# A graph kernel whose matmul groups hand their semaphore updates to TensorE's sequencer

## The reference

```python
# layer 0: spline convolution
messages = jnp.einsum('ek,ei,kio->eo', basis, x[row], weight)   # basis: 9 values per edge
out = zeros.at[col].add(messages) / jnp.maximum(degree, 1.0)[:, None] + x @ root_w.T + root_b
x = _layernorm(x + out)
# layer 1: tensor product with a radial network
R = jax.nn.relu(abs_distances[:, None] @ w1 + b1) @ w2 + b2     # 384 used weights per edge
Y = spherical_harmonics(rel_vec)
msg = ...                          # einsums of R, Y and features[src]
x = _layernorm(x + zeros.at[dst].add(msg))
```

## Time and profile before

| | |
|---|---|
| median of 3 runs | 11,184.96 us (11,180.47 to 11,219.96) |
| profiled execution | 11,204.5 us is its span, from the first to the last instruction; no other time of it is given |
| TensorE busy, matmuls | 7268.4 us, 65%, 30,515 records |
| TensorE weight loads | 3770.5 us, 34%, 30,515 |
| VectorE | 5863.1 us, 52%, 14,800 |
| ScalarE | 2726.5 us, 24%, 7,061 |
| GpSimd | 5939.1 us, 53%, 6,282 |
| mean granted TensorE clock | 0.790 |

### The profile page before, as it was taken

One profiled execution on the slowest core, in us unless ns is written; L12 is line 12 of the kernel. 1 busy time (PEld: TensorE's weight loads), 2 busy tenths in 40 slices (PEclk: granted clock), 3 DMA queues, 4 the chain that ended last, 5 costly groups with the idle time before them and its releaser, 6 DMA issues. The chain is left out here.

```text
span 11204.5 us, 123807 instructions
## 1 busy us (share of the span) xinstructions
PE 7268.4 (65%) x30515; PEld 3770.5 (34%) x30515; DVE 5863.1 (52%) x14800; ACT 2726.5 (24%) x7061; POOL 5939.1 (53%) x6282
## 2 busy tenths in 40 slices
PE   5555555555555555556777777777777777777777
PEld 2222222222222222233333333333333333333334
DVE  3333333333333333335666666666666666666666
ACT  1000000000000000013333333333333333333333
POOL 5555656555555555554444445444445444444443
PEclk8777777777777777778888888888888888888887
DMA  1111111111111111112111111111111111111111
GB/s 26 13 13 13 13 13 13 13 13 13 13 13 13 13 13 13 13 22 50 43 42 42 43 42 44 42 41 43 41 42 44 43 42 41 43 43 42 43 41 38
DMA packets 640988, 332.17 MB, mean 30 GB/s; under 512 B 522497, under 2 KB 573212, under 8 KB 640718
## 3 DMA queue, kind: packets, MB, share of 16 engines
q0 software_dynamic: 200800, 205.61, 9.7%
q10 hardware_dynamic: 266000, 112.04, 4.9%
q1 hardware_dynamic: 174168, 14.29, 1.2%
HBM read 325.06 MB, written 6.40 MB: 30 GB/s over the span
## 5 line engine op out<-in xcount | busy, mean ns | idle before, releaser
L166 POOL DMA_INDIRECT rows<-table_dram,idx_a x1875 | 1778.6, 949 | 2153.3 <-DVE prods L1010 1563.6
L166 POOL DMA_INDIRECT rows<-in_x,idx_a x1890 | 1786.3, 945 | 1072.9 <-issue 547.3
L897 PE MATMUL sums_ps<-prods,hot 128*64 128x272 f32 x12500 | 1817.9, 442 | 697.3 <-DVE acc L1041 356.8
L581 PE MATMUL sums_all<-spread,hot 128*64 128x289 f32 x6250 | 2039.3, 482 | 112.4 <-DVE spread L459 75.1
L886 PE MATMUL radial_x<-w2p,hidden 128*128 128x384 f32 x3750 | 1703.5, 600 | 506.5 <-DVE prods L1010 462.2
L166 POOL DMA_INDIRECT rows<-table_dram,idx_b x1250 | 1182.4, 946 | 1000.4 <-DVE prods L1010 639.5
L166 POOL DMA_INDIRECT rows<-in_x,idx_b x1260 | 1191.0, 945 | 945.9 <-DVE spread L459 575.0
L897 PEld LDWEIGHTS sums_ps<-prods,hot 128*64 128x64 f32 x12500 | 945.2, 152 | 1589.8 <-issue 792.9
L857 ACT ACTIVATE hot<-window,rel_t 128x64 f32<-128x64 f32 x3125 | 812.8, 335 | 2373.4 <-remote 1753.2
L581 PEld LDWEIGHTS sums_all<-spread,hot 128*64 128x64 f32 x6250 | 943.6, 160 | 909.7 <-issue 472.7
L886 PEld LDWEIGHTS radial_x<-w2p,hidden 128*128 128x128 f32 x3750 | 805.3, 230 | 1072.8 <-issue 413.9
(11 more groups left out here) (148 smaller groups left out, 5749.7 us busy)
## 6 DMA issues: line engine op xcount, KB each, us to landing
dist_ab<-in_edge_weight ACTq DMA_DIRECT2D x125, 480.0 KB
dist_ab<-in_edge_weight ACTq DMA_DIRECT2D x125, 320.0 KB
rows<-in_x,idx_a POOLq DMA_INDIRECT x1890
rows<-table_dram,idx_a POOLq DMA_INDIRECT x1875
rows<-in_x,idx_b POOLq DMA_INDIRECT x1260
rows<-table_dram,idx_b POOLq DMA_INDIRECT x1250
vec_s<-in_edge_attr ACTq DMA_DIRECT2D x125, 37.5 KB
idx_a<-in_src SPq DMA_DIRECT2D x251, 7.5 KB
```

Of the source, the lines that this page charges most:

```text
L166: pool.indirect_dma_start(out=rows[u][:, j, 0:width], out_offset=None, in_=table, in_offset=bass.IndirectOffsetOnAxis(ap=idx[u // 3][:, u ...
L581: last = pe.matmul(sums_ps[s][0:WINDOW, 0:K + 1], hot[s][:, j, :], spread[s][:, j, :], start=(j == 0), stop=(j == G - 1))
L897: last = pe.matmul(sums_ps[s][k * WINDOW:(k + 1) * WINDOW, 0:HALF], hot[s][:, j, :], prods[s][:, j, MUL + 16 * k:MUL + 16 * (k + 1), :].re ...
```

## The change

In both loops the last matmul of a group loses its update. Behind each group stands a drain on TensorE, and the semaphore is updated when the drain is done. Nothing else moves: same matmuls, operands, waits and order. The set-up and the transposes between and behind the loops (lines 544 to 568, 630, 1107) keep their updates.

```diff
@@ spline_layer @@
                 for j in range(G):
-                    last = pe.matmul(sums_ps[s][0:WINDOW, 0:K + 1], hot[s][:, j, :], spread[s][:, j, :], start=(j == 0), stop=(j == G - 1))
-                last.then_inc(summed, 1)
+                    pe.matmul(sums_ps[s][0:WINDOW, 0:K + 1], hot[s][:, j, :], spread[s][:, j, :], start=(j == 0), stop=(j == G - 1))
+                pe.drain().then_inc(summed, 1)
...
                 for c in range(3):
-                    last = pe.transpose(fold_ps[SLOT[u]][0:CH + 1, c, :], ...)
-                last.then_inc(folded, 1)
+                    pe.transpose(fold_ps[SLOT[u]][0:CH + 1, c, :], ...)
+                pe.drain().then_inc(folded, 1)
...
-                last.then_inc(msg_ready, 1)
+                pe.drain().then_inc(msg_ready, 1)
@@ tensor_edges @@
-                    last.then_inc(radial_ready[h], 1)
+                    pe.drain().then_inc(radial_ready[h], 1)
...
-                last.then_inc(summed, 1)
+                pe.drain().then_inc(summed, 1)
...
-                last.then_inc(turned, 1)
+                pe.drain().then_inc(turned, 1)
```

More of the change, by code:

```diff
@@ L589, in fold @@
                 for c in range(3):
-                    last = pe.transpose(fold_ps[SLOT[u]][0:CH + 1, c, :], flat[SLOT[u]][:, c * CH:c * CH + CH + 1], ident[0:WINDOW, 0:WINDOW])
-                last.then_inc(folded, 1)
+                    pe.transpose(fold_ps[SLOT[u]][0:CH + 1, c, :], flat[SLOT[u]][:, c * CH:c * CH + CH + 1], ident[0:WINDOW, 0:WINDOW])
+                pe.drain().then_inc(folded, 1)
             def weigh(g):
@@ L597, in weigh @@
                     m = CH + (c == 2)
-                    last = pe.matmul(msg_ps[0:C + 1, 0:U * WINDOW], wk[0:m, c, :], sums[0:m, c, :], start=(c == 0), stop=(c == 2))
-                last.then_inc(msg_ready, 1)
+                    pe.matmul(msg_ps[0:C + 1, 0:U * WINDOW], wk[0:m, c, :], sums[0:m, c, :], start=(c == 0), stop=(c == 2))
+                pe.drain().then_inc(msg_ready, 1)
             with pe.Fori(0, passes) as p:
@@ L885, in radials @@
                     for j in range(tiles):
-                        last = pe.matmul(radial[h][:, j, 0:R], hidden[s][:, (j0 + j) * P:(j0 + j + 1) * P], w2p[:, :],
-                                         start=True, stop=True)
-                    last.then_inc(radial_ready[h], 1)
+                        pe.matmul(radial[h][:, j, 0:R], hidden[s][:, (j0 + j) * P:(j0 + j + 1) * P], w2p[:, :], start=True, stop=True)
+                    pe.drain().then_inc(radial_ready[h], 1)
             def sum_edges(g, u):
@@ L896, in sum_edges @@
                     for k in range(2):
-                        last = pe.matmul(sums_ps[s][k * WINDOW:(k + 1) * WINDOW, 0:HALF], hot[s][:, j, :],
-                                         prods[s][:, j, MUL + 16 * k:MUL + 16 * (k + 1), :].rearrange("e o i -> e (o i)"),
-                                         start=(j == 0), stop=(j == G - 1))
-                last.then_inc(summed, 1)
+                        pe.matmul(sums_ps[s][k * WINDOW:(k + 1) * WINDOW, 0:HALF], hot[s][:, j, :],
+                                  prods[s][:, j, MUL + 16 * k:MUL + 16 * (k + 1), :].rearrange("e o i -> e (o i)"),
+                                  start=(j == 0), stop=(j == G - 1))
+                pe.drain().then_inc(summed, 1)
             def turn(g, u):
@@ L905, in turn @@
                 for k in range(2):
-                    last = pe.matmul(sums_ps[s][k * 32:(k + 1) * 32, TURN:TURN + WINDOW], red[s][:, :], ident[:, k * WINDOW:(k + 1) * WINDOW],
-                                     start=True, stop=True)
-                last.then_inc(turned, 1)
+                    pe.matmul(sums_ps[s][k * 32:(k + 1) * 32, TURN:TURN + WINDOW], red[s][:, :], ident[:, k * WINDOW:(k + 1) * WINDOW],
+                              start=True, stop=True)
+                pe.drain().then_inc(turned, 1)
             with pe.Fori(0, passes) as p:
```

## The result

The changed kernel takes **10,390.3 us** (median of 4, 10,377.9 to 10,426.3) beside 11,189.0 of the kernel before: ratio 0.928, 95% interval 0.9256 to 0.9303, so 7.2% faster. The forecast of 11,980 had the wrong sign. The profiled execution has a span of 10,424.4 us.

A forecast was written before the change was run, and what follows sets the result against it. GpSimd was taken as bound by TensorE completions held until gathers pause. Span 11,204 + 344 (second loop) + 450 (first loop) = 11,998 us, median 11,980; likeliest case 11,300 to 12,900, 8 in 10 from 9,300 to 12,900.

The forecast's parts named there:

- Completions are late while gathers run, and let out by their pauses: Both loops: TensorE's completions reach other engines late until gathers pause; 8.7 us of pauses per first-loop batch.
- A held place counts as not idle, so drains are held as well: TensorE's queue: places held behind finished matmuls make drains equally late; held drains, moderately slower, chance 0.50, 11,980 us.
- The signs set down: Right: drains of several us under gathers, "remote" waits become TensorE waits. Wrong: drains below 0.5 us, product within 0.2 us.
- The first rival, prompt drains: Both loops: drains look only at the array and aren't held; first-loop batch 32 us, 9,340 us in all, chance 0.35.
- The rule on the drain: Skill rule: increment on the matmul, separate barrier by drain waiting for full idleness; 11,980 if held places count, else 9,340.
- The bubble: TensorE's restart gap behind each drain, taken as 0.35 us, between 0.15 and 0.6.
- The chain of a unit: Second loop: four bubbles lengthen TensorE's chain per unit from 6.10 to 7.5 us; VectorE's own is 6.24.
- The first loop: Sums and folds no longer computed early: 3.6 us per batch exposed of 7.6, 450 us in all (0 to 950).
- The second loop: the failed step: Lost running ahead, up to 1.45 us exposed per unit, against added pauses; net 0.55, 344 us (0 to 906).
- counter-effect: Second loop: later VectorE starts gathers later, leaving more pauses with prompt completions; it lowers 1.45 to 0.55 us per unit.
- "no change" rival: Both loops: loss of running ahead and added pauses cancel; 11,185 us, chance 0.08.
- The lower bound of the range, 9,300: Lower end of the 8-in-10 range, set to include the prompt-drains case without its lower half, 0.13.

The follow-up runs named there:

- 5: Kernel before with one gather of a unit's five in both loops, the other rows zeros: 6,158.2 us, ratio 0.5498.
- 4: Kernel before, no drains; in the second loop GpSimd waits for each unit's rows before the next gathers: 0.9394 where completions are late, 1.171 where prompt.
- 7: Drains in the second loop only, plus two or three GpSimd waits for rows per first-loop batch, against the kernel before: 0.8812 and 0.8802.
- 8: Against kernel before: pause3 without the turn's drain, 1.1568 prompt, 0.875 to 0.911 late; pauses in both loops without drains, 1.2796 prompt, 0.9276 late.
- 6: Kernel before with second-loop drains of one kind: behind radial groups 10,918.6 us (0.9884), behind the sum 10,429.8 to 10,676.6 us.
- after_again: The changed kernel run once more beside the kernel before, completions late: 10,361.2 us against 11,194.7, ratio 0.9263.
- l1_only: The change's drains in the first loop only, second loop as in the kernel before, completions prompt: 8,026.1 us, ratio 1.0005.
- l2_only: The change's drains in the second loop only, first loop as in the kernel before: 8,693.4 us (1.0836) where prompt; 10,025.6 us (0.8952) where late.
- radial_drain: Kernel before with a drain behind each radial group alone, two per unit of the second loop, completions late: 10,918.6 us, ratio 0.9884.
- pause3: Drains in the second loop only, plus three GpSimd waits for rows per first-loop batch, against the kernel before, completions late: 9,724.7 us, 0.8802.
- both_b: Kernel before with updates kept on the matmuls and a bare drain behind each group, completions late: 10,241.1 us, ratio 0.9146.
- spaced_l2_b: Kernel before, no drains; GpSimd waits in the second loop for each unit's rows before the next gathers, completions late: 10,524.8 us, 0.9394.

## Why the prediction was wrong

*Completions are late while gathers run, and let out by their pauses.* Right as to the gathers (5), and as to what enough pauses do (4, 7, 8), and the whole case hangs on it. Two things were missing. In the long bursts of the first loop many completions come out without a pause (139 of the 300 counted above), and a pause under 1.2 us mostly lets nothing out (6). Nor is it a constant of the machine: in the prompt condition gathers run without a pause and nothing is late.

*A held place counts as not idle, so drains are held as well.* This was the step trusted least, and it held: 13 us in the first loop's timeline, and in the second the sum's drain, 2.88 us in the median against 2.45 in the prompt condition. The signs set down came mixed: drains of up to 18.3 us and waits for TensorE in place of "remote" in the first loop, as for right; a product 0.12 us behind its matmuls in the second, as for wrong. The first rival, prompt drains, came out right in sign and not in its mechanism: its first loop of 32 us and 9,340 in all didn't come.

*The rule on the drain.* The Trainium skill (PSUM — Partial Sum Buffer, section Engine vs sequencer instructions) asks for the increment on the matmul itself, or on a drain where a barrier of its own is wanted. It calls that a matter of correctness and names no price, so no time here speaks for or against it. That a drain waits until the engine is fully idle is borne out as far as the first loop's drains, held like the matmuls' own completions, go.

*The price of drains.* It hangs on the condition: four a unit in the second loop took 8.4% more in the prompt one and 10.5% less in the late one.

*The bubble.* Taken as 0.35, measured as 0.37 for the turn's. The chain of a unit: 7.5, measured 7.44, both in the prompt condition.

*The first loop.* +450 us forecast, +360 measured (in after_again a batch takes 41.9 us, which makes it some +280), by the mechanism named: the work that ran early into the held stretch now waits behind a held drain.

*The second loop: the failed step.* The prediction put the exposed part at "1.45 per unit" and went on: "Against it, a VectorE that is later starts gathers later, which leaves more pauses with prompt completions; from below nothing." The counter-effect was seen, and given no more than the loss itself: the sum took 0.55 us net, so 0.9 of gain against 1.45 of loss. Measured is -1.85 us per unit in place of +0.55, some 1,500 us of the total, so the gain was at least 1.85.

The reading that fits all runs is this. Without drains a unit of TensorE's and VectorE's work takes 6.37 us (l1_only), hardly more than its five gathers' 6.24. So the gathers hardly pause: in the late condition the kernel before issues two units' gathers in a row, or with a pause under 1.2 us between them. What TensorE completes late in this stretch is then held, for 7 to 9 us in the earlier trace rows, and a pause of over 5 us follows, 281 times in 619 units.

With four bubbles the work of a unit takes 7.44 us, 1.2 more than its gathers. That alone makes a pause behind every unit, 1.4 us in the prompt condition and 1.9 in the late one (607 of the changed kernel's 615 lie between 1.2 and 3 us), and it comes before anything but the sum is held. The bubbles are a brake that keeps the loop out of the state in which it loses 3 us. That the pauses gain is shown (4: no drain, 0.939), and so is that four drains make them (l2_only, where nothing is held); that a pause must be over 1.2 us or so to count is read from the rows in 6 and no run sets it. That the clock rose to 1.00 goes with it: in the earlier trace rows TensorE stood idle for 5.99 us and the sum behind it took 4.25 us, the lower level; in the rows of the changed kernel the idle times are 0.2 to 0.7 us and a sum takes 2.51.

The "no change" rival named the deciding point ("where the added pauses give back more than the exposed part") and priced it at 0. The lower bound of the range, 9,300, came from another mechanism, and the time lay in the range by that luck.

*Open:* what makes a chip late or prompt (five sets against two; the only chip known to have come twice was late both times), and what the holding counts. In the first loop of the changed kernel, of the drains whose group ended within a burst, none of 582 was late by more than 0.1 us where the group ended up to 4.5 us behind the burst's start, 137 of 170 were between 5 and 6.5 us, and all 193 beyond. But time, gathers and matmuls since the start grow together in these runs, and in radial_drain the count runs on over pauses under 1.2 us. What lets completions out in the middle of a long burst is open too.

Of the versions tried, pause3 has the lowest median in the late condition, 12% below the kernel before and 5% below the changed one. In the prompt condition nothing beat the kernel before: drains in the second loop cost 8%, pauses there 17%, and pauses in both loops 28%.

## What to carry to other kernels

Where a profile shows an engine's results reaching others late only while another engine issues without a break, look at its breaks, their lengths above all (the mere number misled here): a brake on the issuer, or a bubble that acts as one, can be worth more than the work it delays, and a feedback of this kind must not be bounded at zero. Before building on such an effect, look whether it is there on another chip: here the second loop's drains are -10% on one and +8% on another. A drain behind a short group on TensorE cost about 0.37 us of its chain here where nothing hid it, and nothing measurable where TensorE was idle anyway (1.0005).

## What the runs showed of the hardware

The same kernel took 8,012 to 8,025 us on two chips and 11,033 to 11,196 on the others. In the second loop without drains (before and l1_only) a gather took 0.945 and 0.944 us in the median and VectorE's product of one tile 0.546 and 0.535; what differs is when TensorE's completions reach others under gathers, and with it TensorE's clock (0.84 and 1.00). A drain waits for completions that are late in this way, and a matmul's own update is about as late as one behind a drain (18.2 us in the mean at the additions of both_b, 19.6 in the changed kernel). The release came 2.3 to 2.6 us behind the start of a burst's last gather in the second loop (7900.27 to 7902.57, 8017.85 to 8020.49), and anywhere from the middle of the burst to 4.9 us behind its last gather in the first (1216.81 to the addition at 1221.70). GpSimd's wait for the rows of its own unit cost a pause of 2.2 us or more, 2.36 in the median (spaced_l2_b).
